# Block attention with a linear layer, one core: copy, transposing DMA and join of the probabilities by head instead of by pair of heads

## What is computed

```
def attention(h):                        # h = layernorm(x)
    q, k, v = (split_heads(h @ W + b) for W, b in ((Wq, bq), (Wk, bk), (Wv, bv)))   # 16 heads of 64
    # local: a block of 128 queries sees the 256 keys from 64 before it to 64 behind it
    probs = softmax(where(valid, q_block @ k_window.T / 8, -1e9))
    ctx = probs @ v_window
    # global: 64 queries of each head (first, last, the 62 with the largest norm of q) see all 1024 keys
    ctx[idx] = softmax(q[idx] @ k.T / 8) @ v
    return ctx
x = x + attention(layernorm(x))
x = x + layernorm(x) @ (weight * scale_weight[:, None]).T + bias
```

## Time and profile before

| what | value |
|---|---|
| median of 3 runs | 2273.47 us (2257.78 to 2281.11) |
| the profiled execution, its own time | 2270.97 us |
| its span, first to last instruction | 2269.4 us |
| TensorE matmuls busy | 2077.3 us (92%) |
| VectorE busy | 1533.3 us (68%) |
| ScalarE busy | 999.8 us (44%) |
| GpSimd busy | 611.0 us (27%) |
| granted TensorE clock, mean | 0.947 |
| the chain that ended last | PE 36%, DMA 24%, DVE 18%, ACT 11%, issue 7% |

### The profile page before, as it was taken

One profiled execution on the slowest core, in us unless ns is written; L12 is line 12 of the kernel. 1 busy time (PEld: TensorE's weight loads), 2 busy tenths in 40 slices (PEclk: granted clock), 3 DMA queues, 4 the chain that ended last, 5 costly groups with the idle time before them and its releaser, 6 DMA issues.

```text
span 2269.4 us, 35082 instructions
## 1 busy us (share of the span) xinstructions
PE 2077.3 (92%) x11264; PEld 1725.3 (76%) x11264; DVE 1533.3 (68%) x2747; ACT 999.8 (44%) x1275; POOL 611.0 (27%) x474
## 2 busy tenths in 40 slices
PE   6998889989988899899898898999988989999999
PEld 6877777777777677678676787887777878888887
DVE  5687766663877666546877576657666777666664
ACT  4316555573245555553365465623646655000000
POOL 2342123114331232124331321254223112222211
PEclk9998999989989998899899898999999989999999
DMA  3436776544366665453475765524766656333331
GB/s 131 115 111 141 135 115 142 107 98 130 103 141 132 114 142 124 100 118 111 104 156 130 124 132 110 123 85 100 135 129 146 145 102 174 141 124 134 139 135 69
DMA packets 534555, 280.68 MB, mean 124 GB/s; under 512 B 434000, under 2 KB 499606, under 8 KB 534416
## 3 DMA queue, kind: packets, MB, share of 16 engines
q1 hardware_dynamic: 506896, 188.83, 39.2%
q0 software_dynamic: 23200, 74.53, 11.1%
q10 hardware_dynamic: 4320, 15.73, 1.7%
HBM read 122.73 MB, written 51.44 MB: 77 GB/s over the span
## 4 chain that ended last, share of the span: by engine, by line
PE 36%; DMA 24%; DVE 18%; ACT 11%; issue 7%; SPq 3%; DVEq 0%; ACTq 0%; POOL 0%; POOLq 0%
DMA p_turned<-p_parts 20%; PE proj L802 14%; PE proj L642 13%; ACT pT L1130 6%; DVE p_parts L1495 4%; DMA v_turned<-q_sq 4%; ACT pT_g L1130 3%; PE pv L760 3%; DVE top_val L1450 2%; DVE top_idx L1452 2%; DVE x_norm L1454 2%; SPq L289 2%; DVE q_sq L1416 1%; PE pv L782 1%; PE turn L791 1%
## 5 line engine op out<-in xcount | busy, mean ns | idle before, releaser
L642 PE MATMUL proj<-xT_hi,w_hi 128*128 128x512 f32 x1536 | 427.6, 423 | 9.6 <-DVE kT_lo L1435 9.5
L642 PE MATMUL proj<-xT_hi,w_lo 128*128 128x512 f32 x1536 | 428.0, 409 | 0.0
L642 PE MATMUL proj<-xT_lo,w_hi 128*128 128x512 f32 x1536 | 393.0, 399 | 1.0 <-DVE xT_lo L1410 1.0
L1495 DVE COPY p_parts<-probs 128x2048 uint16<-128x2048 uint16 (+1 forms) x160 | 244.1, 1526 | 221.6 <-DMA p_turned<-p_parts 190.1
L451 POOL CAST w_hi<-w_raw 128x1024 fp32r<-128x1024 f32 x96 | 107.2, 1117 | 1059.1 <-PE proj L642 822.1
L1130 ACT COPY pT<-p_turned 128x2048 uint16<-128x2048 uint16 x128 | 323.5, 2528 | 122.3 <-DMA p_turned<-p_parts 121.3
L760 PEld LDWEIGHTS pv<-v_nat,pT 128*128 128x128 f32 x2048 | 273.6, 211 | 122.5 <-issue 100.9
L760 PE MATMUL pv<-v_nat,pT 128*128 128x65 f32 x2048 | 276.9, 294 | 96.3 <-ACT v_nat L1095 54.1
L642 PEld LDWEIGHTS proj<-xT_lo,w_hi 128*128 128x128 f32 x1536 | 297.3, 194 | 69.2 <-DVE xT_lo L1410 2.3
L642 PEld LDWEIGHTS proj<-xT_hi,w_hi 128*128 128x128 f32 x1536 | 291.7, 200 | 72.6 <-DVE kT_lo L1435 10.3
L642 PEld LDWEIGHTS proj<-xT_hi,w_lo 128*128 128x128 f32 x1536 | 290.0, 195 | 61.8
(11 more groups left out here) (176 smaller groups left out, 2949.9 us busy)
## 6 DMA issues: line engine op xcount, KB each, us to landing
w_raw<-in_wstream POOLq DMA_DIRECT2D x96, 512.0 KB, 4.2
x_buf<-in_rows SPq DMA_DIRECT2D x47, 512.0 KB, 3.4
q_rows<-pT SPq DMA_DIRECT2D x64, 256.0 KB, 2.3
ctx_rows<-ctx_out SPq DMA_DIRECT2D x128, 128.0 KB, 2.6
out<-q_store ACTq DMA_DIRECT2D x30, 512.0 KB, 2.7
q_store<-in_cols POOLq DMA_DIRECT2D x28, 512.0 KB, 5.5
q_store<-ctx_rows SPq DMA_DIRECT2D x28, 512.0 KB, 4.1
q_store<-in_rows SPq DMA_DIRECT2D x8, 512.0 KB, 6.7
```

What stands on the lines that cost most here:

```text
L642: mm = pe.matmul(proj[:, bank, :], w[b][:, k * P:k * P + P], x[:, k, half * HALF:half * HALF + HALF], start=(m == 0), stop=(m == 23), skip ...
L1495: dve.tensor_copy(p_parts[:, 0:2 * words].rearrange("p (s x) -> p s x", s=2), probs[:, 0:words].bitcast(U16).rearrange("p (x s) -> p s x", ...
```

## The change

Four things are done, all in the loop over pairs unless said otherwise.

1. The copy, the transposing DMA and the join of each step are cut in two, one for each head. The first half covers the first 512 words of `probs` (8 blocks of 128 x 128), the second the other 512 (in the global step 640, 10 blocks). Each half has its own semaphore for the landing, and p_parted and pT_set count halves. TensorE waits for the first half ahead of the first head's 8 matmuls, and for the second ahead of the other 8; the global weighing waits for both.
2. ScalarE writes the join of each half between the exponentials of the next step: exponentials of head 0, join of the half 0 of the step before, exponentials of head 1, join of half 1. For step 1 this puts the join ahead of the output of V (L1078). VectorE puts some work between the two copies of a step.
3. The third V piece of a pair is copied and transposed inside that pair, behind step 0, instead of at the end of the pair before; some stores of SyncE move behind V transposes; gq_lo comes ahead of split_q.
4. Two loads of rows of the next batch come earlier or from GpSimd's queue, with the moments that read them moved likewise, and the first two weight slices are loaded by SyncE behind the first rows instead of by GpSimd at the start.

The core of the diff. Its parts are, in order, SyncE's transposes, TensorE's weighing, `attend` of ScalarE, `attend` of VectorE, and SyncE's weight loads ahead of the loop over batches:

```diff
             def turn_p(n, hp, s):
...
-                i, words = n * (PAIRS * EVENTS) + hp * EVENTS + s, words_of(s)
-                sp.wait_ge(p_parted, i + 2)
-                apart(sp)
-                sp.wait_ge(pT_set, i + 1)
-                apart(sp)
-                sp.dma_start_transpose(p_turned[:, 0:2 * words].rearrange("p (x r) -> p x r", r=P),
-                                       p_parts[:, 0:2 * words]).then_inc(p_moved, 16)
+                i = n * (PAIRS * EVENTS) + hp * EVENTS + s
+                for h in range(2):
+                    words = half_words(s, h)
+                    sp.wait_ge(p_parted, 2 * i + h + 3)
+                    apart(sp)
+                    sp.wait_ge(pT_set, 2 * i + h + 1)
+                    apart(sp)
+                    sp.dma_start_transpose(p_turned[:, 2 * words.start:2 * words.stop].rearrange("p (x r) -> p x r", r=P),
+                                           p_parts[:, 2 * words.start:2 * words.stop]).then_inc(p_moved[h], 16)
...
             def weigh(u, s):
...
-                pe.wait_ge(pT_set, u * EVENTS + s + 2)
                 for h in range(2):
+                    pe.wait_ge(pT_set, u * (2 * EVENTS) + 2 * s + h + 3)
...
             def attend(n, hp, following=True):
...
                 for h in range(2):
                     exps(u, 0, h)
+                    if not opens:
+                        join_p(n, hp - 1, STEPS, (h,))
                 if ahead:
                     ahead_hi(1)
-                if not opens:
-                    join_p(n, hp - 1, STEPS)
                 columns(0)
                 for h in range(2):
                     exps(u, 1, h)
-                join_p(n, hp, 0)
+                    join_p(n, hp, 0, (h,))
...
                 exps(u, 3, 0)
                 gq_hi_out(u)
+                join_p(n, hp, 2, (0,))
                 exps(u, 3, 1)
-                join_p(n, hp, 2)
+                join_p(n, hp, 2, (1,))
...
             def attend(n, hp, half, top=(), following=True):
...
-                part_p(n, hp, 0)
+                part_p(n, hp, 0, 0)
                 if ahead:
                     ahead_lo(1)
+                part_p(n, hp, 0, 1)
+                part_v(n, hp, 2)
                 if hp > 0:
                     pv_out(u - 1, 3)
...
+                gq_lo_out(u)
                 if not last:
                     split_q(u + 1, hp + 1)
-                gq_lo_out(u)
...
-                if not last:
-                    part_v(n, hp + 1, 2)
-                part_p(n, hp, STEPS)
+                for h in range(2):
+                    part_p(n, hp, STEPS, h)
                 pv_out(u, 2)
...
+            for b in range(2):
+                sp.dma_start(w_raw[b][:, :], wstream[b]).then_inc(raw_first[b], 16)
```

More of the change, by code:

```diff
@@ L141, in build @@
         raw_in = [sem(f"raw_in{b}") for b in range(2)]
+        raw_first = [sem(f"raw_first{b}") for b in range(2)]
         w_hi_set = sem("w_hi_set")
@@ L361, in stores @@
                 turn_p(n, hp, 2)
-                store_ctx(n, hp, 0)
                 if not last:
                     turn_v(n, hp + 1, 0)
+                store_ctx(n, hp, 0)
                 turn_p(n, hp, 3)
+                if not last:
+                    turn_v(n, hp + 1, 1)
                 if hp == HALF_PAIRS - 1:
@@ L445, in split @@
             def split(n, i, b, count, bank=None, done=None):
-                pool.wait_ge(raw_in[b], 16 * count + 16)
+                if isinstance(count, int) and count == 0:
+                    pool.wait_ge(raw_first[b], 16)
+                else:
+                    pool.wait_ge(raw_in[b], 16 * count)
                 if bank is not None:
@@ L592, in batch @@
                         store_rows(n, 1)
+                    if hp == 0 and following:
+                        load_rows(n, 3)
                     if hp == 1:
@@ L1114, in global_exps, with join_p @@
                 act.wait_ge(max_set, u * (2 * EVENTS) + 2 * EVENTS)
-                act.wait_ge(p_parted, u * EVENTS + STEPS + 1)
+                act.wait_ge(p_parted, u * (2 * EVENTS) + 2 * STEPS + 2)
                 g = 4 * STEPS
                 act.activation(probs[:, HD:HD + SEQ], score[:, :], ACT.Exp, bias=neg_max[:, g:g + 1]).then_inc(exp_set, 2)
-            def join_p(n, hp, s):
-                i, words = n * (PAIRS * EVENTS) + hp * EVENTS + s, words_of(s)
-                act.wait_ge(p_moved, 16 * i + 32)
-                if s in (2, 3):
-                    act.wait_ge(pv_done, i - 1)
-                elif isinstance(hp, int) and hp == 0 and s == 0:
-                    for h in range(2):
+            def join_p(n, hp, s, halves=(0, 1)):
+                i = n * (PAIRS * EVENTS) + hp * EVENTS + s
+                for h in halves:
+                    words = half_words(s, h)
+                    act.wait_ge(p_moved[h], 16 * i + 32)
+                    if h == 0 and s in (2, 3):
+                        act.wait_ge(pv_done, i - 1)
+                    elif isinstance(hp, int) and hp == 0 and s == 0:
                         act.wait_ge(q_stored[h], n * (16 * PAIRS) + 16 * PAIRS + 16)
                         act.wait_ge(q_squared[h], n * PAIRS + PAIRS + 1)
-                apart(act)
-                act.copy(pT_of(s)[:, 0:words].bitcast(U16).rearrange("p (x s) -> p s x", s=2),
-                         p_turned[:, 0:2 * words].rearrange("p (s x) -> p s x", s=2)).then_inc(pT_set, 1)
+                    apart(act)
+                    act.copy(pT_of(s)[:, words].bitcast(U16).rearrange("p (x s) -> p s x", s=2),
+                             p_turned[:, 2 * words.start:2 * words.stop].rearrange("p (s x) -> p s x", s=2)).then_inc(pT_set, 1)
             def lin_hi(t, b):
@@ L1752, in batch @@
                             top_find(n, 0, step)
-                if following:
-                    row_moments(n, 1)
+                        if following and r == 5:
+                            row_moments(n, 1)
                 top_rows(n, 0)
```

69 lines of the change are left out of this document (32 added, 37 removed).

## The result

| | before | after |
|---|---|---|
| median of 4 runs each | 2275.77 us | 2132.95 us |
| lowest to highest | 2257.78 to 2281.11 | 2114.69 to 2139.30 |
| profiled execution, its own time | 2270.97 us | 2139.30 us |
| its span | 2269.4 us | 2137.7 us |
| mean granted clock | 0.947 | 0.968 |

The ratio of after to before is 0.9371, with a 95% interval of 0.9305 to 0.9437: the changed kernel is 6.3% faster. The forecast was 2152 us in a range of 2095 to 2230; the measured median lies 19 us under the forecast and inside the range.

A forecast was written before the change was run, and what follows sets the result against it. TensorE's own work was the floor, with 208 us of waits and slow-clock matmuls above it. Savings of 30 + 40 + 10 + 8 + 16 = 104 us, times 1.42, less 28, made 120: forecast 2152 us, range 2095 to 2230.

The forecast's parts named there:

- Place one: Border between two pairs: moving the third V piece saves 30 us of ctx_out waits and 40 of pT_g waits.
- The fear that step 0's transposes would meet the load: Border between pairs: the possible failure, step 0's transposes meeting GpSimd's weight load, with other TensorE work before they are needed.
- Place two: Pair before the last: joining step 1 ahead of the V output saves 10 us of V waits and 8 of pT.
- Place three: Opening pairs and pairs with statistics: halving shortens each chain before V by 2 us, 16 in all (0 to 24).
- The factor of 1.42: TensorE: each microsecond of wait costs another 0.42 us in matmuls at the lower clock, so saved waits count times 1.42.
- The charge: Loop over pairs: 28 us for added half copies, joins, DMA issues and new waits, with ends of 0 and 100.
- The start: Kernel start: first two weight loads go behind the input rows on SyncE, counted as 0, between -4 and +4 us.
- Its marks: Signs of being right in the new profile: limits on waits, transpose time, pair times and clock in the four stretches.
- Serial: Step transposes: the second half pays its 3.2 us after the first, 6.4 instead of 4.5; 2346 us, chance 0.08.
- VectorE takes over: VectorE: copies fall behind and half of the 104 us comes back at other places; 2225 us, chance 0.16.
- Nothing arrives: Steps and borders: second halves land as the whole did, collisions move to step 0; 2260 us, chance 0.08.
- Everything arrives: TensorE's waits: all 146 us but 25 of the opening chains go, without charge; 2099 us, chance 0.10.

The follow-up runs named there:

- the V piece alone: Kernel before with plain DMAs for the transposing ones and only the third V piece moved behind step 0: 2136.09 us, ratio 0.9421.
- the other reorderings: Changed kernel with plain DMAs and every reordering, but copy, DMA and join whole: 2144.04 us, ratio 0.9458; compared with only the V piece moved.
- the stand-ins: Three whole-kernel runs with every transposing DMA replaced by a plain one, data moved but not turned: 2109.36, 2136.09 and 2144.04 us.
- The stand-in of after: Changed kernel with every transposing DMA replaced by a plain one, copies, joins and bytes kept: 2109.36 us, ratio 0.9295.
- the chain alone: Only copy, plain DMA and join, without the attention: a round takes 7.84 us whole, 6.26 in halves; beside GpSimd 8.8 and 8.7.

## Why the prediction was right, and where it was not

**The place and the mechanism.** Place one was named as the largest term, and the V piece alone does most of the work: an estimated 109 of 125 us by the split above. The forecast for this place was (30 + 40) x 1.42 = 99. Within it the terms were off in both directions. pT_g lost all of its 50.4 us where 40 were forecast. ctx_out lost 6.3 (33.5 to 19.0 and 8.2) where 30 were forecast: this is the term that failed most. The V piece did take it away (1.8 us left at that line), but ahead of the global weighing 8.2 are new, and the other reorderings go with 11.1 us more on the stand-ins. The stand-in of after has 18.9 of ctx_out in all and the changed kernel 27.2; which 8.3 us those are wasn't looked into. One reading of the prediction does not fit its own rows: it has the global copy start at 377.5, 1.6 us before the 379.13 of the earlier trace rows, and counts 2.3 us less queue. The fear that step 0's transposes would meet the load came true and cost TensorE nothing at the clean border: they are issued at 1126.69 for 5.12 us, behind two loads of GpSimd (1125.73 and 1126.58), and ScalarE joins the first at 1133.13 after a wait of 0.88.

**Place two** was right for V. The wait in the pairs before the last went from 4.3 us in each of four batches to 1.97 in three and 1.88 in the fourth, 9.4 us in all (10 forecast). The stand-ins show that this is the order of the join and not the halving, as the prediction had it: 4.3 with the V piece alone, 1.97 with the join ahead, whole or in halves. For pT the number was right and the reason is not shown: it lost 7.9 (8 forecast), but with the V piece and the plain DMA the waits in these pairs are gone without the new order of the join. The new wait for gq_hi was named there too, at "about 1 us a pair"; at this place it is 4.46, and TensorE waits 2.5 behind it.

**Place three** was mis-sized. 16 us were forecast for the opening pairs and the pairs with the statistics; those eight waits fell from 36.9 to 33.8, by 3.1. On the stand-ins halving took 5.8 us from all waits for V, those put down to "issue" included (31.0 to 25.2), so the chains became less than 1 us shorter each and not 2. In batch 3, which has no following batch to load, the opening wait fell from 5.19 to 1.88. In batch 0 it grew from 7.59 to 10.50. The timeline of the changed kernel there:

```profile
165.68 2.34 POOL L456 TENSOR_TENSOR w_lo<-w_raw,w_hi 128x1024 fp32r<-128x1024 f32 x1
...
165.90 2.67 DVE L1503 COPY p_parts<-probs 128x1024 uint16<-128x1024 uint16 x1 [0.35 <-DVE x_norm L1461]
...
168.62 0.57 POOL L464 DMA_DIRECT2D w_raw<-in_wstream  x1 [0.61 <-POOL w_lo L456]
...
172.50 1.34 ACT L1136 COPY pT<-p_turned 128x1024 uint16<-128x1024 uint16 x1 [5.91 <-DMA p_turned<-p_parts]
...
179.67 1.35 ACT L1136 COPY pT<-p_turned 128x1024 uint16<-128x1024 uint16 x1 [3.64 <-DMA p_turned<-p_parts]
```

A half copy begins beside GpSimd's subtraction and takes 2.67 us instead of 0.69. Its transpose is issued at 168.81, behind the load of weights (168.62) and two loads of the next batch's rows (162.55), and ScalarE waits 5.91 and again 3.64 us. In the stand-in of after GpSimd's subtraction begins at 167.03, when the copy of the first half is long done (165.36, 0.70 us), and TensorE waits 2.72. The prediction counted 0 for the moved row loads, as they "lie beside projections", and had no such collision in these chains. How much of the 10.5 us is the copy's and how much the loads' is open: a version with the loads later wasn't run.

**The clock.** The factor of 1.42 rested on a floor of 38.6 us for a pair. The undisturbed pair after takes 37.2, so more of the excess was slow clock than the prediction counted: by its own sum with 37.2 the excess is 248 us and the factor 1.69. 76 us of waits went, and 124.7 us of time: 1.63 for each. The clock in the four stretches is 0.94, 0.94, 0.95 and 0.97, where 0.95 or more was forecast: two are below.

**The charge** of 28 us for what the change adds wasn't found as such. The joins of halves take 1370 ns, as interpolated (1.37), the half copies 834 (0.90 or less), although some are still caught beside GpSimd: their median is 694. VectorE has 14 us more work and not 30, ScalarE in sum none. What came instead were ctx_out waits and, on the stand-ins, busy time at the lower clock. So 76.6 x 1.63 = 125 stands where 104 x 1.42 - 28 = 120 was forecast: the sum was right by luck, with errors of both signs. Its terms hold for the pair before the last and roughly for pT_g, not for ctx_out, the opening pairs, the factor of the clock and the charge. The start gave 6 us more than the 0 forecast, past the bound of 4.

**Its marks.** No ctx_out wait behind a 3.5 us global copy: right. pT_g under 12 us: right, none. Pair before the last under 48 us: right, 45.70. Seven pairs of a batch in 288 us: 287.0 on average, from 301.2 down to 272.5. Transposes near 3.2 us: the first half at the border above was there at most 3.7 us after its issue (1121.22 to 1124.92, with a wait of 0.41); no median is to be had, since two are under way at a time.

**The rivals.** *Serial* is out: at the border above the second half, of ten blocks, was there 5.6 us after the first one's issue at the latest, where the rival had 6.4; ScalarE's waits fell from 209 to 73 us, where it had them grow by 120; and in the chain alone a second plain half came within 1.3 us of the first. The Trainium skill (DMA: Bandwidth & Descriptors, Rules for kernel authors) says of two transfers to disjoint partition halves that they serialize. Here the halves are columns, and the prediction carried the rule over to them; by it the round in halves would not have been shorter, and it was by 1.6 us. So for halves in columns and the plain DMA the rule does not hold; halves of partitions were run nowhere here, and for the transposing DMA only the traces of the changed kernel speak. The rival's point of no gain was a little off as well: by its own terms, (85 - 28 - 40) / (100 x 0.54 x 1.42) + 0.7, it is a second half 0.9 us later, not 0.8. *VectorE takes over* happened in part: the ctx_out waits of 2.5 and 2.8 us behind the opening pair (at 194.85, 237.82 and 681.80 us) end stretches in which VectorE is not idle for more than half a microsecond at a time, with the next batch's statistics among its work (2.5 us at 184.57 and 227.54). In batch 3, without these statistics, no such wait is over 0.5 us there (0.46 at 1532.95). *Nothing arrives* is out. *Everything arrives* (2099) fell short by the waits that are left.

## What to carry to other kernels

When one copy stands in front of a chain that feeds the bounding engine, look first at where it stands and not at how long it is: moving a single 0.9 us copy and its transfer out from ahead of the global step brought most of a 6% gain, by an estimate that gives 17 to 38 us to the plain DMA. At the borders one sees why: the next copy came out from beside a neighbour's subtraction and its transfer away from a load. Halving a transfer pays about 1.6 us a round where the pieces overlap, and nothing where the halved copies run beside GpSimd. After a reordering, list what is queued behind each new wait, and which of it was ready: gq_lo ahead of the split of q put 1.9 us of ready work behind a 4.5 us wait, but the second of the copies behind it got its own input only 0.2 us before the first began. And count the waits and the slow matmuls apart: the other reorderings left TensorE's idle time as it was and still cost 13 us.

## What the runs showed of the hardware that was not expected

A copy of VectorE that starts while GpSimd's subtraction runs makes hardly any way until the subtraction ends. The whole global copy before ended at 382.69, 1.22 us behind the subtraction's end at 381.47, about what such a copy takes alone (1.36 in the run with the V piece alone). The half copy of the changed kernel ended at 168.57, 0.55 behind 168.02, and the second half copy of the chain alone 0.55 behind; a half copy takes 0.65 to 0.69 us alone. So a copy that is caught waits for the rest of the subtraction, whole or half, and two halves can be caught twice. The Trainium skill (SBUF — State Buffer, Who interferes with whom) describes it, for VectorE instructions in its 2-port mode, as a lock that the first of VectorE and GpSimd holds for its whole instruction while the other fully blocks; the three ends above agree with that, and no run here shows the mode. The prediction counted 2.0 us for this copy at each border; it did not count that halves can be caught one after the other. How much of the gain lies in the copy alone was not measured apart.

The issue of a transposing DMA held SyncE's queue for 1.95 us in the median for 16 blocks, and that of a plain one of the same bytes for 0.60; from copy to join the two were nonetheless within 0.2 us in the median.
